# A relational graph-attention layer on one core: splitting the group norm of four late node blocks

## The reference

```python
for r in range(R):                                   # 5 edge types
    q, k, v = x[dst] @ W_Q[r], x[src] @ W_K[r], x[src] @ W_V[r]
    logits = (q * k).sum(-1) / 4 + attn_bias[r]      # per head
    attn = segment_softmax(logits, dst, edges of type r)
    out += segment_sum(attn * v, dst)
out = out @ out_proj_w.T + out_proj_b
h = out + x
y = (h - mean(h)) / sqrt(var(h) + 1e-5) * ln_gamma + ln_beta
result = layernorm(x + y)
```

## Time and profile before

| | before |
|---|---|
| median of 3 runs | 1106.9 us (1106.75 to 1107.29) |
| profiled execution, own time | 1108.52 us |
| profiled execution, span | 1106.0 us |
| VectorE busy | 979.8 us, 89% |
| POOL busy | 761.6 us, 69% |
| TensorE busy | 770.6 us, 70% |
| ScalarE busy | 518.6 us, 47% |
| granted TensorE clock, mean | 0.765 |

### The profile page before, as it was taken

The page is one execution under the profiler, slowest core; times in us unless marked ns, Lnnn a source line. Parts: engine busy times, 40 slices in busy tenths (PEclk is TensorE's granted clock), DMA queues, the critical chain, the costliest instruction groups (busy, mean ns, idle before and its releaser), DMA issues.

```text
span 1106.0 us, 17147 instructions
## 1 busy us (share of the span) xinstructions
PE 770.6 (70%) x4312; PEld 684.5 (62%) x4312; DVE 979.8 (89%) x1834; ACT 518.6 (47%) x960; POOL 761.6 (69%) x859
## 2 busy tenths in 40 slices
PE   9945576667776676766677776777777656776575
PEld 4524466566666666665677665676667646766475
DVE  2725789899999999899999999999999899999997
ACT  4634444444454454444455444454444444545322
POOL 1047777777777777777777777777777777777750
PEclk9976578778877778776877777877876777777776
DMA  8986566665666656566665656766556556656500
GB/s 325 371 274 199 175 194 198 180 175 163 174 186 185 178 171 176 169 181 166 189 184 178 183 175 166 201 181 175 164 175 172 170 153 171 167 170 170 159 28 13
DMA packets 121368, 198.62 MB, mean 180 GB/s; under 512 B 22845, under 2 KB 79546, under 8 KB 121166
## 3 DMA queue, kind: packets, MB, share of 16 engines
q0 software_dynamic: 37632, 102.81, 32.9%
q1 hardware_dynamic: 79602, 85.54, 25.5%
q10 hardware_dynamic: 4032, 9.13, 2.3%
HBM read 170.49 MB, written 26.89 MB: 178 GB/s over the span
## 4 chain that ended last, share of the span: by engine, by line
DVE 48%; issue 25%; DMA 10%; PE 8%; POOL 4%; DVEq 3%; ACT 1%; SPq 1%; POOLq 0%; ACTq 0%
DMA ring<-KVtab,kvi 8%; DVE LT L1317 7%; DVE pool L1380 6%; DVE pool L1409 6%; DVE av L670 5%; DVE pool L1281 4%; DVE pool L1303 4%; POOL ring L1692 4%; PE pp L567 3%; DVE Tt L1293 3%; DVE Yt L1366 3%; DVE ohn L650 2%; DVE Mt L1395 2%; PE pp L1840 2%; DVE aggT L1258 2%
## 5 line engine op out<-in xcount | busy, mean ns | idle before, releaser
L1692 POOL DMA_INDIRECT ring<-KVtab,kvi x784 | 744.2, 949 | 303.7 <-issue 226.1
L1799 PE MATMUL pp<-qwin,pool 128*128 128x128 f32 x1568 | 276.0, 333 | 63.4 <-DVE pool L1303 40.3
L1799 PEld LDWEIGHTS pp<-qwin,pool 128*128 128x128 f32 x1568 | 250.4, 242 | 81.0 <-issue 60.0
L1857 PE MATMUL pp<-ohn,av 128*128 128x128 f32 x1464 | 225.7, 314 | 14.7 <-DVE av L670 14.5
L1857 PEld LDWEIGHTS pp<-ohn,av 128*128 128x128 f32 x1464 | 218.1, 233 | 18.6 <-DVE av L670 18.6
L1840 PE MATMUL pp<-sel,pool 120*128 120x96 f32 (+1 forms) x536 | 141.7, 443 | 78.8 <-DVE av L670 76.7
L1840 PEld LDWEIGHTS pp<-sel,pool 120*128 120x128 f32 (+1 forms) x536 | 128.5, 324 | 97.5 <-issue 95.2
L1303 DVE TENSOR_TENSOR pool<-pp,ring 128x512 f32<-128x512 f32 x196 | 132.9, 678 | 55.3 <-DMA ring<-KVtab,kvi 31.7
L1815 PE MATMUL LT<-ident,LM 128*120 128x128 f32 (+1 forms) x268 | 56.3, 348 | 163.3 <-DVE Yt L1366 159.7
L886 ACT ACTIVATE pool<-rkb,npid 128x512 bf16<-128x512 bf16 x196 | 139.7, 713 | 52.5 <-DMA rkb<-Ktab 49.8
L913 ACT ACTIVATE Et<-pool 120x512 f32<-120x512 f32 (+1 forms) x66 | 41.6, 631 | 247.7 <-DVE pool L1281 247.7
(11 more groups left out here) (128 smaller groups left out, 691.3 us busy)
## 6 DMA issues: line engine op xcount, KB each, us to landing
rkb<-Ktab SPq DMA_DIRECT2D x196, 128.0 KB
mk<-Mtab SPq DMA_DIRECT2D x201, 100.2 KB
KVtab<-pool SPq DMA_DIRECT2D x25, 640.0 KB, 5.6
ring<-KVtab,kvi POOLq DMA_INDIRECT x784
qwin<-Qfast SPq DMA_DIRECT2D x196, 64.0 KB
Qfast<-pool ACTq DMA_DIRECT2D x21, 320.0 KB, 3.2
xs<-in_x_b SPq DMA_DIRECT2D x5, 320.0 KB, 4.5
out<-hb SPq DMA_DIRECT2D x24, 64.0 KB, 2.6
```

The lines of the kernel that those rows point to most:

```text
L1692: e.indirect_dma_start(kv[:, home(m), j, :], None, KV, bass.IndirectOffsetOnAxis(kvi[:, 4 * q + j:4 * q + j + 1], 0)).then_inc(kv_in[m % 6 ...
L1799: last = e.matmul(pp[2 + m % 2][:, j * C:(j + 1) * C], ohr[:, m % OR, j * C:(j + 1) * C], qwin[:, m % 3, :], start=True, stop=True)
L1857: last = e.matmul(fourfold(f)[:, :, 0:n], weighed_at(f)[:, j, :], hot_at(f)[:, j, None, 0:n].broadcast_to([128, 4, n]), start=(j == 0), st ...
```

## The change

The table of sizes is changed so that the group of blocks 15 to 18 becomes three groups: 15 alone, 16 alone, and 17 with 18. The groups after it get higher numbers, and the list of the late roots and `root_count` follow.

```diff
-LATE_ROOTS = [(4, 1), (5, 1), (6, 1), (4, 2), (5, 2), (6, 2), (7, 1), (8, 1), (9, 1), (7, 2), (8, 2), (9, 2)]
+LATE_ROOTS = [(6, 1), (7, 1), (8, 1), (6, 2), (7, 2), (8, 2), (9, 1), (10, 1), (11, 1), (9, 2), (10, 2), (11, 2)]
 
 
 def root_count(g, k):
 
-    return 2 * g + k if g < 4 else 9 + LATE_ROOTS.index((g, k))
+    return 2 * g + k if g < 6 else 13 + LATE_ROOTS.index((g, k))
...
-SIZES = (5, 5, 5, 4, 1, 1, 1, 1, 1, 1)
+SIZES = (5, 5, 5, 1, 1, 2, 1, 1, 1, 1, 1, 1)
```

## The result

| | before | after |
|---|---|---|
| median of 22 runs each, same chip | 1106.74 us (1104.34 to 1111.02) | 1109.08 us (1106.07 to 1114.6) |
| ratio after / before | | 1.0025, 95% interval 1.0017 to 1.0034 |
| profiled execution, own time | 1108.52 us | 1107.91 us |
| profiled execution, span | 1106.0 us | 1106.2 us |
| VectorE busy | 979.8 us | 984.3 us |

The kernel became slower by 2.8 us by the ratio (1.9 to 3.8). I had forecast 1107.2 us, no change, with 1108.6 as the upper end. The forecast was wrong: what the change moves on VectorE cost about what was worked out, and a collision that I had not looked for took almost four microseconds in step 193.

The account below looks back on a forecast made before the run. VectorE was taken as the bound from step 161 to the end. The terms 0 + 0.25 + 0 + 0, rounded to +0.3 us, on the median 1106.9 gave 1107.2 us; range 1106.0 to 1108.6.

Parts of the forecast that it names:

- VectorE's moved work: Norm work of 2.9 us moves from steps 189 to 191 into 165, 166, 178 and 179; net 0.
- The wait of `scaled`: In step 165, VectorE's `scaled` of block 15 waits for ScalarE's root, +0.25 us, bounds 0 to 0.6.
- The other roots: Four more ScalarE roots, with TensorE waiting for keys at 165, 178 and 188, hidden from VectorE: 0, up to 0.3 us.
- B: Rival: keys late behind roots and outputs at three places; slower, 1110.2 us, or 1112.3 at most; chance 0.08.
- C: Rival: moved norms in steps 165 and 178 fall into waits for gathers; 2.9 us faster, 1104.3 us; chance 0.05.
- D: Rival: another TensorE clock level in the tail, 1085 to 1090; up to 2.2 us less, 1105.0 us; chance 0.07.
- SyncE's queue: Early outputs ahead of loads of quads 170, 183 and 193 cost 0; quad 195's load some 2 us earlier gains 0.
- The load's price: A keys load on SyncE takes 4.05 us from issue by the trace, 2.3 us by a page's fit; same sum.

Follow-up runs that it names:

- e3: Kernel before, with SyncE issuing only the load of quad 195's keys ahead of the four outputs of step 191; ratio to before 1.0024.
- f1: Changed kernel, with GpSimd's first three weighings also waiting for the scan of turn 63 (its running maximum); ratio to before 1.0028.
- f2: Changed kernel, with GpSimd's weighings waiting for turn 63's running maximum and its six features for turn 63's shift; ratio to before 1.0018.
- g2: Changed kernel, with turn 63's two shift pieces swapped and GpSimd's weighings waiting for the backward scan of turn 63; ratio to before 1.0000.
- e5: Changed kernel, with the two shift pieces of turn 63 swapped, on a chip where before takes 1290.4 us; ratio to before 1.0011.
- e1: Changed kernel, with GpSimd's first three weighings waiting until the shift of turn 63 is done; ratio to before 1.0004.
- e1c: Changed kernel, with GpSimd's first three weighings waiting for turn 63's shift, run again on the chip of f1, f2 and f3; ratio to before 0.9996.
- g1: Changed kernel, with SyncE holding back the load of quad 195's keys until the logits of step 192; ratio to before 1.0000.
- e2: Kernel before, with GpSimd's first three weighings waiting until the shift of turn 63 is done; ratio to before 1.0000.
- e6: Changed kernel, with GpSimd's second and third weighings and features waiting for turn 63's 120x64 shift piece, where before takes 1290.4 us; ratio to before 1.0008.
- a0: Changed kernel run again, nothing added, on a chip where before takes 1109.1 us; ratio to before 1.0027.
- f3: Changed kernel, with turn 63's two shift pieces swapped and GpSimd's weighings waiting for turn 63's running maximum; ratio to before 1.0030.
- a1: Changed kernel run again, nothing added, on a chip where before takes 1285.6 us; ratio to before 1.0009.
- e7: Changed kernel with another split, 15 with 16 and 17 with 18, on a chip where before takes 1290.4 us; ratio to before 1.0010.
- e7b: Changed kernel with the split 15 with 16 and 17 with 18, on a chip where before takes 1285.6 us; ratio to before 0.9999.
- e5b: Changed kernel, with the two shift pieces of turn 63 swapped, on a chip where before takes 1285.6 us; ratio to before 0.9998.

## Why the prediction was wrong

**VectorE's moved work, 0 net: right.** 1.78 us late at step 167 (1.5 and the wait forecast), 3.24 at step 180 (2.9 and the wait), 0.32 at step 192.

**The wait of `scaled`, +0.25: right.** 0.23 us, from a root that stood back to back as in the earlier trace rows: its second half ended 0.62 us behind the start of the larger root's second half.

**The other roots, 0: right in the sum, wrong in a detail.** VectorE never waited for keys or queries. I expected TensorE to wait for line 890 at two or three places; the waits from 905 to 1045 list one of 2.6 us, as before.

**Rivals B and C did not happen, D not in this execution.** No load came too late, no moved norm fell into a wait for a gather, and from 1085 to 1090 the granted clock was 0.50 as in the earlier trace rows. But what D says of the tail does occur: the time from step 194 to the end was 48.2 to 48.3 us in e3, f1, f2 and g2, where from 25 to 30 us behind step 194 the granted clock was 0.60 to 0.63 instead of 0.50, and 50.5 in e5, where from 40 to 44 us behind it the clock was 0.50 instead of 0.73. So single profiles differ by up to 2.3 us there.

**SyncE's queue, 0: this is the term that failed.** I wrote that the load of quad 195 may come some 2 us earlier and that "nothing on VectorE waited for it, so that gains 0". The load did come 2.7 us earlier against step 193. But I asked only who waits for it, not what it starts. The chain is load, keys(195), `keep_weights` behind it on ScalarE, GpSimd's weighings; the last wait of the earlier trace rows, 4.19 us for this very load, was what had kept GpSimd's 5.5 us clear of VectorE's one short instruction with two tensors in SBUF. The bound of that term should have reached to +5.5, the length of GpSimd's batch; it measured +3.83 in the profiled execution. e3 (the early load alone does it: 1.0024 against 1.0027 for the whole change on the same chip) settles this, e1 and e1c show that it goes by way of GpSimd, and g1 (all but the early load: 1.0000) agrees, on a chip of its own.

A page read against these rows would have warned: the Trainium skill, "SBUF — State Buffer", section "SBUF: two separate sides", says that VectorE and GpSimd share one pair of ports under an exclusive lock, taken by whoever starts first when a VectorE instruction has two SBUF inputs and GpSimd reads SBUF, and that the other "fully blocks". The traces agree on who is held (two SBUF tensors 4.11 us, one in PSUM 0.67) and on first come (g1). On how long they agree in e2 and e6, where the hold ended with the weighing that it met, and differ elsewhere: the page has the lock held for one instruction, a weighing lasts 1.03 us here, and the piece took up to 4.39.

**The load's price.** Beside the 4.05 us of its rows the prediction sets an estimate of 2.3 us. The Trainium skill, "DMA: Bandwidth & Descriptors", section "Anatomy of one DMA — SWDGE (gpsimd) path", gives the fit behind it for transfers on GpSimd's path, and this load is issued by SyncE. In the changed kernel the loads from 1026 to 1041 us landed 3.6 us after their issue. The sum went by the 4.05, so nothing changes in it.

**What stays open.** In every profile in which the piece met the first or second weighing in the old order of pieces, with the features behind, step 193 was 3.8 to 4.1 us longer, and 0.32 come from the rest, so some 4.1 to 4.4 would be due; the runs give 2.8 (1.9 to 3.8) and 3.0 (1.8 to 4.1 in a0). Three things may lie between: some executions miss the collision; some of before have it, in step 193, where GpSimd stood clear by 0.15 us, or in the last turn's `shift`, where the margin was smaller still; and the clock in the tail gives back about half a microsecond in some profiles (e3, f1). Single profiles can't tell their shares. Nor is it settled what decides over how many GpSimd instructions a hold goes.

## What to carry to other kernels

A transfer or instruction that comes earlier can cost time: follow it forward to every engine that it releases, and set what that engine then does against what runs beside it. VectorE instructions with two tensors in SBUF and batches on GpSimd are better kept apart in time, and where a kernel is tuned, a wait that looks idle may be what keeps them apart. Such a collision shows in no list of waits; look for a form whose duration has grown.

## What the runs showed of the hardware

- A VectorE instruction of 0.27 us with two tensors in SBUF took up to 4.39 us beside back-to-back GpSimd instructions of 1.03 us (weighings) and 0.42 us (features). Held for however long, it ended each time about 0.1 us behind the end of one of them: the first (e2 and e6, last turn), the second (g2), the third (f2, f3, e5), the eighth (a0, e3, f1), the ninth (after, a1). The wait for one of them to end would be 1.03 us at most.
- Beside the features alone the same form took 0.31 us (e7, e7b) and 0.53 us (e5b), far less than beside weighings.
- One SBUF tensor is not held: the 120x448 piece (0.67 us) and line 1317 (0.67 us at 1048.86, beside the first two weighings) kept their times.
- GpSimd is slowed too: beside VectorE's scans over two SBUF tensors (`mk` and another) three weighings took 4.92 us instead of 3.09, in the kernel before as in the changed one. The scan of line 1409 took 1.89 us there; elsewhere it takes 1.28, but with its mask in PSUM, and no profile has the form with both in SBUF and 512 columns by itself.
- The kernel before took 1107 to 1109 us on some chips and 1286 to 1290 on two others. In the changed kernel (after and a1) the gathers have the same mean time on both kinds, 948 and 951 ns, but 301 and 480 us of idle time ahead of them. Why is not shown.
